# Values of the second and third layers projected with the tokens down the partitions

## The reference, cut to what matters

```python
# layer 1: xf is the normalized input, (2, 2048, 1024) before; heads of 64
v = jnp.einsum('bnd,hed->bhne', xf, Wv)
p = jax.nn.softmax(s, axis=-1)
return jnp.einsum('bhqk,bhke->bhqe', p, v)
...
# layer 2
qkv = hidden_states @ qkv_w + qkv_b
q, k, v = (qkv[0], qkv[1], qkv[2])
...
attn = jax.nn.softmax(attn, axis=-1)
out = attn @ v
return out @ proj_w + proj_b
```

## Time and profile before

| | |
|---|---|
| median of 3 runs | 1311.58 us (1311.43 to 1311.86) |
| profiled execution, its own time | 1311.57 us |
| its span, first to last instruction | 1309.8 us |
| mean granted TensorE clock | 0.993 |
| TensorE matmul busy | 1273.7 us, 97% of the span |
| VectorE, ScalarE, GpSimd busy | 768.2, 435.7, 644.4 us |

### The profile page before, as it was taken

One profiled execution on the slowest core, in us unless ns is written; L12 is line 12 of the kernel. 1 busy time (PEld: TensorE's weight loads), 2 busy tenths in 40 slices (PEclk: granted clock), 3 DMA queues, 4 the chain that ended last, 5 costly groups with the idle time before them and its releaser, 6 DMA issues.

```text
span 1309.8 us, 19974 instructions
## 1 busy us (share of the span) xinstructions
PE 1273.7 (97%) x7216; PEld 1022.7 (78%) x7216; DVE 768.2 (59%) x1579; ACT 435.7 (33%) x1101; POOL 644.4 (49%) x726
## 2 busy tenths in 40 slices
PE   5999889999999999999999999999999999999998
PEld 4888676478888888888888778787877787778787
DVE  7424433866675515667442788877267887767222
ACT  3511132034443301444330345434024444343212
POOL 4632189255555565555556444445654445564000
PEclk9999989999999999999999999999999999999999
DMA  5211014022222232222233232322323323220011
GB/s 176 87 42 47 25 45 119 9 61 74 79 67 75 71 97 82 74 73 74 73 88 97 79 87 74 99 79 78 106 79 93 87 75 98 71 73 1 9 57 65
DMA packets 83296, 96.33 MB, mean 74 GB/s; under 512 B 24960, under 2 KB 46112, under 8 KB 83200
## 3 DMA queue, kind: packets, MB, share of 16 engines
q1 hardware_dynamic: 82048, 92.97, 24.3%
q10 hardware_dynamic: 1152, 2.10, 0.5%
HBM read 82.45 MB, written 8.39 MB: 69 GB/s over the span
## 4 chain that ended last, share of the span: by engine, by line
PE 81%; DVE 3%; issue 2%; ACT 1%; POOL 0%; ACTq 0%; DVEq 0%; POOLq 0%
PE PS L1102 52%; PE PS L1633 5%; PE PS L1142 4%; PE PS L1165 4%; PE PS L928 3%; PE PS L1181 2%; PE PS L935 2%; PE PS L941 2%; PE PS L1191 2%; PE PS L1650 2%; PE PS L1210 2%; PE PS L1156 1%; DVE part L411 1%; DVE part L1606 0%; ACT part L406 0%
## 5 line engine op out<-in xcount | busy, mean ns | idle before, releaser
L1102 PE MATMUL PS<-XB,w_hi 128*128 128x512 f32 x1024 | 349.9, 401 | 1.2 <-POOL w_lo L220 1.2
L218 POOL CAST w_hi<-w_raw 128x512 fp32r<-128x512 f32 x195 | 124.9, 640 | 335.0 <-PE PS L1102 232.3
L220 POOL TENSOR_TENSOR w_lo<-w_raw,w_hi 128x512 fp32r<-128x512 f32 x195 | 256.9, 1317 | 15.6
L1102 PEld LDWEIGHTS PS<-XB,w_hi 128*128 128x128 f32 x1024 | 192.3, 188 | 43.7 <-issue 2.2
L1102 PE MATMUL PS<-XB,w_lo 128*128 128x512 f32 x512 | 199.6, 390 | 0.0
L1309 ACT ACTIVATE part<-PS,nmax 128x256 f32<-128x256 f32 (+1 forms) x256 | 112.1, 445 | 253.9 <-DVE nmax L1413 128.2
L1102 PE MATMUL PS<-XB,part 128*128 128x512 f32 x768 | 195.1, 397 | 0.0
L1102 PEld LDWEIGHTS PS<-XB,part 128*128 128x128 f32 x768 | 140.0, 188 | 28.9
L1423 DVE TENSOR_SCALAR part<-part,prec 128x256 f32<-128x256 f32 (+1 forms) x256 | 138.3, 581 | 4.5
L220 POOL TENSOR_TENSOR part<-part,part 128x512 fp32r<-128x512 f32 x85 | 113.0, 1330 | 6.8
L218 POOL CAST part<-part 128x512 fp32r<-128x512 f32 x85 | 53.8, 633 | 121.3 <-PE PS L1102 111.3
(11 more groups left out here) (140 smaller groups left out, 2007.9 us busy)
## 6 DMA issues: line engine op xcount, KB each, us to landing
w_raw<-in_w SPq DMA_DIRECT2D x187, 256.0 KB, 2.6
part<-in_w SPq DMA_DIRECT2D x85, 256.0 KB, 2.6
strips<-part SPq DMA_DIRECT2D x16, 256.0 KB, 2.3
out_x<-xT SPq DMA_DIRECT2D x16, 256.0 KB, 2.1
part<-strips SPq DMA_DIRECT2D x128, 24.0 KB
xT<-in_x ACTq DMA_DIRECT2D x8, 256.0 KB, 7.7
xT<-in_x SPq DMA_DIRECT2D x8, 256.0 KB, 10.0
w_raw<-in_w SPq DMA_DIRECT2D x16, 128.0 KB, 3.1
```

Source lines behind the costliest of these rows:

```text
L218: pool.tensor_copy(hi, raw).then_inc(w_hi_done, 1)
L220: pool.tensor_tensor(lo, raw, hi.bitcast(F32), ALU.subtract).then_inc(w_ready, 1)
L1102: m = nc.tensor.matmul(PS[:, bank, :], wt[:, (c % 4) * P:(c % 4) * P + P], rhs(hl, c), start=c == k == 0, stop=c == CK - 1 and k == 2)
```

## The change

The normalized input becomes the stationary side of the value projection, and the weights stream. For each of the four groups of 128 tokens, each of the eight chunks and each of the three products there is one matmul: 128 x 128 of `XB` stationary, 128 columns of weights streaming. The result lies in the bank as `v` needs it, so `turn_values`, `take_v` and `vT` go; ScalarE copies the bank straight to `v`, which now has two buffers. The value has bank 7 for all items. The query no longer waits for the value's evacuation. The bias of layer 2's values is added after attention instead (`evac_o`, `rest_of_o`; the rows of a softmax sum to one). `rest_of_o` moves behind `normalize(i, 0)` on VectorE. Query and key are projected as before.

```diff
-    PJ = {"Q": 0, "K": 1, "V": 0}
+    PJ = {"Q": 0, "K": 1, "V": 7}
-    def bank_of(i, kind):
-        return PT if (i, kind) == (0, "V") else PJ[kind]
...
+        def values_of(i, c, h):
+            n = slots[(i, "V"), c // 4]
+            _, hi, lo = w_slot(n)
+            if c % 4 == 0:
+                pe.wait_ge(w_ready, n + 1)
+            for tt in range(4):
+                for k, (wt, hl) in enumerate(((hi, 0), (lo, 0), (hi, 1))):
+                    m = nc.tensor.matmul(PS[:, PJ["V"], tt * P:tt * P + P], x_part(hl, h, c)[:, tt * P:tt * P + P],
+                                         wt[:, (c % 4) * P:(c % 4) * P + P], start=c == tt == k == 0,
+                                         stop=c == CK - 1 and k == 2, skip_group_check=True)
+            if c % 4 == 3:
+                m.then_inc(w_used[slot_of[n]], 1)
...
                 if c == 0 and kind == "Q":
-                    pe.wait_ge(v_evac, i)
+                    pe.wait_ge(q_hi, i)
+                    pe.wait_ge(q_lo, i)
+                    if i > LO_KEYS:
+                        pe.wait_ge(rel_evac, 2 * (i - LO_KEYS))
...
-                if i and c == 0 and kind == "V":
-                    pe.wait_ge(q_hi, i + 1)
-                    pe.wait_ge(q_lo, i + 1)
+                if c == 0 and kind == "V":
+                    pe.wait_ge(v_ready, i)
                     if layer_of(i) == 2:
                         pe.wait_ge(rel_evac, 2 * (i - LO_KEYS) + 2)
+                    if i % PAIRS == 1 and i > PAIRS:
+                        pe.wait_ge(sum_done, CK * (i // PAIRS))
                 if i == c == 0:
-                    evacuated(pe, len(groups) - 8 + bank_of(i, kind))
+                    evacuated(pe, len(groups) - 8 + PJ[kind])
...
-                if c == 0 and o == 1 and s in (1, 2):
-                    pe.wait_ge(rel_evac, 2 * PAIRS * (s - 1) + 2)
+                if c == 0 and o == 1 and s < 3:
+                    pe.wait_ge(v_ready, PAIRS * (s + 1) + 1)
...
             scores(i, 0)
-            project(i + 1, "Q", range(0, 4))
-            turn_values(i)
-            project(i + 1, "Q", range(4, CK))
+            project(i + 1, "Q", range(CK))
...
         def evac_v(i):
             product_done(act, (i, "V"))
-            if i:
-                act.wait_ge(v_tr, i)
...
+            if i >= 2:
+                act.wait_ge(o_done, 2 * i - 2)
+            nc.scalar.activation(v[i % 2].rearrange("p a n -> p (a n)"), PS[:, PJ["V"], :], ACT.Copy).then_inc(v_ready, 1)
...
             maxima(i, 0)
+            normalize(i, 0)
             if j:
                 rest_of_o(i - 1)
-            normalize(i, 0)
-            take_v(i)
```

More of the change, by code:

```diff
@@ L755, in later_layers @@
     both_rel = carve(11776, [P, 2, 2, SIDE, SIDE])
-    v = carve(12800, [P, 4, P])
-    vT = carve(13312, [P, HALF])
+    v = [carve(12800 + HALF * i, [P, 4, P]) for i in range(2)]
     prob = carve(13824, [P, 4, 2, N])
@@ L791, in later_layers @@
     dve_evac = sem("dve_evac")
-    v_evac = sem("v_evac")
-    v_tr = sem("v_tr")
     v_ready = sem("v_ready")
@@ L1116, in project @@
                     pe.wait_ge(k_lo, i)
-                if i and c == 0 and kind == "V":
-                    pe.wait_ge(q_hi, i + 1)
-                    pe.wait_ge(q_lo, i + 1)
+                if c == 0 and kind == "V":
+                    pe.wait_ge(v_ready, i)
                     if layer_of(i) == 2:
                         pe.wait_ge(rel_evac, 2 * (i - LO_KEYS) + 2)
+                    if i % PAIRS == 1 and i > PAIRS:
+                        pe.wait_ge(sum_done, CK * (i // PAIRS))
                 if i == c == 0:
-                    evacuated(pe, len(groups) - 8 + bank_of(i, kind))
+                    evacuated(pe, len(groups) - 8 + PJ[kind])
                 if i % PAIRS == 0 and kind == "Q":
                     norm.ready(i // PAIRS, c)
-                chunk_of((i, kind), c, lambda hl, c: x_part(hl, h, c), bank_of(i, kind))
+                if kind == "V":
+                    values_of(i, c, h)
+                else:
+                    chunk_of((i, kind), c, lambda hl, c: x_part(hl, h, c), PJ[kind])
         def scores(i, a):
@@ L1181, in attend @@
                         m = nc.tensor.matmul(PS[64 * hh:64 * hh + 64, O, a * N:a * N + N],
-                                             v[:, 2 * a + kt_, 64 * hh:64 * hh + 64],
+                                             v[i % 2][:, 2 * a + kt_, 64 * hh:64 * hh + 64],
                                              probT[:, (n0 + hh) % 4, kt_ * N:kt_ * N + N], start=kt_ == 0, stop=kt_ == 1)
@@ L1203, in relative @@
             pe.wait_ge(v_ready, i)
+            if i % PAIRS == 1:
+                pe.wait_ge(sum_done, CK * (i // PAIRS))
             pe.wait_ge(tables_ready, 1)
@@ L1361, in evac_o @@
             hi, src = o_parts(i)[0], o_source(i)
-            nc.scalar.activation(hi, src, ACT.Copy).then_inc(o_hi, 1)
+            if layer_of(i) == 1:
+                ins = nc.scalar.activation(hi, src, ACT.Copy)
+            else:
+                ins = nc.scalar.activation(hi, src, ACT.Identity, bias=bias[:, 16 + j:17 + j])
+            ins.then_inc(o_hi, 1)
         evac_q(0)
@@ L1425, in normalize @@
                 last.then_inc(p_norm, 1)
[L1427 to L1431, removed]
         def rest_of_q(i):
@@ L1471, in rest_of_o @@
             (hi, lo), src = o_parts(i), o_source(i)
-            nc.vector.tensor_tensor(lo, src, hi.bitcast(F32), ALU.subtract).then_inc(o_lo, 1)
+            if layer_of(i) == 1:
+                ins = nc.vector.tensor_tensor(lo, src, hi.bitcast(F32), ALU.subtract)
+            else:
+                j = i % PAIRS
+                ins = nc.vector.scalar_tensor_tensor(lo, src, bias[:, 16 + j:17 + j], hi.bitcast(F32), ALU.add, ALU.subtract)
+            ins.then_inc(o_lo, 1)
         def add_out(s, o):
```

## The result

The changed kernel takes 1466.45 us (median of 4, 1465.99 to 1467.3) against 1311.71 for the kernel before: ratio 1.1182, interval 1.1165 to 1.1199, slower. The profiled execution spans 1465.5 us, 155.7 more than before.

The account below looks back on a forecast made before the run. TensorE's instruction stream was taken to bound the kernel; 149.1 us for the items plus 2.4, 1.0 and 0.9 gave 153.4 us on 1311.57, so 1465 us. Range 1434 to 1500 us, held at 85%.

Parts of the forecast that it names:

- The pace of the new matmul: Value projection: each 128 x 128 load outlasts its 128-column matmul and sets 0.110 us, bounds 0.100 to 0.120.
- Net per item: TensorE, each item: value projection +5.10 us, dropped turning -0.44, together +4.66 us; +149 us over 32 items.
- Loads aren't shared: Value projection: every matmul has its own load, so the two products sharing `x_part(0)` save nothing.
- The turning: TensorE, each item: four transposes of the value go, -0.44 us.
- Nothing beside TensorE: ScalarE and VectorE bound no item, so VectorE's saved copy of 0.69 us an item brings zero.
- the 3.4 us for turned probabilities: TensorE's own waits over the whole program: 3.4 us in five waits for turned probabilities, the others less.
- Item 0: First item's value: TensorE stands 3.6 us until bank 7's add ends, 1.23 us of weight waiting given back, net +2.4.
- clock: After the first item's stand: granted clock at the lower level, bounds 0 and 1.7 us, taken as +1.0.
- Cover lost: First item of two later stages: turned probabilities already late, so the 0.44 us gain isn't had there, +0.9 us.
- its fall: Rival: granted clock drops during the value matmuls, 31 drops of 1.7 us, 53 us more, about 1518 us; chance 7%.
- Hidden loads: Rival, value matmuls: loads hide in part, pace between 0.067 and 0.100 us; 1333 us at 0.067, 1388 at 0.085; 6%.
- free loads: Rival, value matmuls: loads cost nothing and the fixed 0.013 us goes, 0.055 us a matmul, about 1296 us; chance 2%.

Follow-up runs that it names:

- e1: Changed kernel with each value matmul loading only 64 of its 128 tokens as stationary side, still streaming 128 columns: 1311.91 us, ratio 0.9997 to the kernel before.
- e2: Changed kernel with each value matmul streaming only 64 of its 128 weight columns against the full stationary side: 1624.57 us, ratio 1.2376 to the kernel before.
- e9: Changed kernel with the old value projection put back, values left unturned, and the first item's value in bank 4: 1296.15 us, ratio 0.9879 to the kernel before.
- e8: Changed kernel with each value matmul streaming 96 of its 128 weight columns: 1606.18 us, two runs.

## Why the prediction was right

- **The pace of the new matmul** (0.110, bounds 0.100 and 0.120): 0.111. It rested on one pair of loads 0.11 us apart and the bound from 256 columns; e1 and e2 show that it is the load, as the prediction had it. Net per item 4.66 was predicted; 96 x 0.111 - 5.46 - 0.44 is 4.76, times 32 three us more than forecast.
- **Loads aren't shared** between products with the same stationary side: 9392 loads for 9392 matmuls.
- **The turning** (-14.1): e9 gives 15.8, with 14 inside its interval.
- **Nothing beside TensorE**: VectorE's 26 us bought nothing; e9 leaves 1.7 us by the medians (-0.2 to 3.9) for all other terms together, item 0's bank apart.
- **A misreading that did no harm**: the prediction calls the 3.4 us for turned probabilities TensorE's largest wait of the whole program. It waited longer in layer 0, 13.0 us on line 661, 5.8 on line 928 and 4.3 on line 696. These stand ahead of the change and are the same after it (13.0, 5.8, 4.3); from 262 us on, 3.4 is the largest.
- **Item 0** (+2.4, clock +1.0): the mechanism was right, the clock's price was too low, 3.4 us against at most 1.7. The stand of 3.5 us was as forecast (3.6), and 1.0 of the forecast 1.23 came back; the trace has 5.8 in all. I took the low clock's price from the last layer, where it ended sooner.
- **Cover lost** (+0.9): the waits for turned probabilities went from 3.4 to 3.9 us, +0.5.
- The errors of +3 and +2.4 were partly met by -1.6 in the last layer, which nothing in the change caused. So 1465 against 1466.45 is closer than the terms were, and that closeness is luck.
- **Rivals.** The clock held at 128 columns; I had put 7% on its fall, with the argument that the new stream has no waits. That argument is wrong: the clock fell without any wait in e2 and e8. So this part of the forecast came true without its reason, and what kept the clock up at 128 columns isn't shown. The price of 53 us was also too low, near 140 to 158, since a fall often lasted 8 us or more and slowed the value's own matmuls too. Hidden loads and free loads (rivals 2 and 3) were refuted by 0.111; in bfloat16 the pace is 0.057, near rival 3's 0.055.

## What to carry to other kernels

Which operand is stationary sets how many loads there are: price a matmul as the larger of its load and its stream, and find the load's price where two loads follow each other with nothing to stream between. Here, for float32r operands, a 128 x 128 load takes as long as some 265 streamed columns (0.111 us at the 0.418 ns a column of the prediction), so turning a [128, 512] result (0.44 us) was far cheaper than projecting it in pieces of 128 columns (5.2 us more an item). When a layout change frees a second engine, look first whether that engine was the limit, and when a bank is reassigned, look at which engine empties it, and when. Look also for single drops of the clock before a difference of 1 or 2 us between two executions is given a cause.

## What the runs showed of the hardware, unexpected

- Loads follow the granted clock: at 0.50 twelve value matmuls took 2.68 us (0.223 each), at 1.00 1.29 to 1.33 (0.11). The Trainium skill ("TensorE: Matmul & The Clock Gate", section on loading the stationary operand) gives the columns over 1.2, 107 ns for 128; the trace agrees at full clock only.
- The clock fell to 0.50 with TensorE never idle, in the runs with 64 and 96 streamed columns behind 128-column loads (1624.57 and 1606.18 us), and not with 112 or 128 (1466.24 and 1466.45; there, from item 0 on, it dropped only at item 0's stand). Why, the runs don't show. Doing less in each matmul cost 140 to 158 us.
- A 64-column load lets a 128-column float32r matmul run at 0.060 us, below the 0.067 that the longer matmuls suggest.
- Behind the same wait of 2.2 us in the last layer, the same 96 matmuls took 23.6 to 23.7 us in seven profiled executions and 22.1 in six.
